# Attention score maxima of the last four heads, taken one pipeline step later, with all working banks in one ring

## The reference

```
x = x + layernorm(attention(layernorm(x)))
x = x + layernorm(ffn(layernorm(x)))

attention, for each batch and head (64-row blocks; d = 16):
  q, k, v = heads(x @ Wq.T + bq), heads(x @ Wk.T + bk), heads(x @ Wv.T + bv)
  first and last block of q: softmax over all of k
  the other blocks: softmax over the first, the last and the neighbouring blocks
  ctx = softmax(q k^T / sqrt(d)) v
ffn: abel = gelu(x @ abel_w + b); logits = x @ gate_w + b; the top two experts per token,
  each gelu(x @ w1 + b1) @ w2 + b2, weighed, rotated by three matrix exponentials and mixed with abel
```

## Time and profile before

| | |
|---|---|
| Median of 3 runs | 1895.45 us (1894.34 to 1897.08) |
| Span of the profiled execution | 1898.1 us |
| PE busy | 1572.6 us (83%) |
| DVE busy | 1247.2 us (66%) |
| ACT busy | 902.9 us (48%) |
| POOL busy | 706.7 us (37%) |
| Mean granted TensorE clock | 0.948 of full speed |

### The profile page before, as it was taken

One profiled execution on the slowest core, in us unless ns is written; L12 is line 12 of the kernel. 1 busy time (PEld: TensorE's weight loads), 2 busy tenths in 40 slices (PEclk: granted clock), 3 DMA queues, 4 the chain that ended last, 5 costly groups with the idle time before them and its releaser, 6 DMA issues. The chain is left out here.

```text
span 1898.1 us, 33342 instructions
## 1 busy us (share of the span) xinstructions
PE 1572.6 (83%) x10429; PEld 1070.8 (56%) x10430; DVE 1247.2 (66%) x3665; ACT 902.9 (48%) x1769; POOL 706.7 (37%) x716
## 2 busy tenths in 40 slices
PE   3988898888888888889888888749999999999700
PEld 1534455454455455545445545548888888888600
DVE  5656767877777787777778673426565555655377
ACT  1145656755756656666666656213333332323234
POOL 0011224324423423432433333414444444445458
PEclk9899999999999999999999999869999999999955
DMA  3331343353244245325424422755655656656387
GB/s 95 111 112 43 93 134 103 102 161 124 96 147 155 88 126 159 111 93 162 131 70 157 143 69 90 245 157 99 145 125 116 142 105 141 134 104 123 45 287 245
DMA packets 184011, 241.46 MB, mean 127 GB/s; under 512 B 23048, under 2 KB 154512, under 8 KB 183760
## 3 DMA queue, kind: packets, MB, share of 16 engines
q1 hardware_dynamic: 157008, 203.57, 33.6%
q0 software_dynamic: 26880, 36.33, 11.5%
HBM read 133.40 MB, written 105.91 MB: 126 GB/s over the span
## 5 line engine op out<-in xcount | busy, mean ns | idle before, releaser
L949 ACT ACTIVATE pexp<-scT 128x512 f32<-128x512 f32 x768 | 439.8, 600 | 322.2 <-PE scT L736 313.3
L1109 DVE TENSOR_REDUCE mx<-work 128x1 f32<-128x320 f32 (+2 forms) x1024 | 492.1, 549 | 48.5 <-PE work L716 46.1
L1599 POOL DMA_INDIRECT y_rows<-rows_add,row_of x144 | 226.8, 1575 | 296.1 <-DMA y_rows<-rows_add,row_of 211.3
L716 PE MATMUL work<-w 126*128 126x320 bf16 (+4 forms) x1280 | 265.1, 299 | 42.9 <-DVE mx L1109 33.6
L736 PE MATMUL scT<-w 128*128 128x192 bf16 (+3 forms) x1536 | 271.7, 275 | 28.2 <-ACT pexp L949 27.3
L1631 PE MATMUL h_ps<-inT,w1c 128*128 128x256 f32 x1152 | 263.6, 382 | 2.4 <-DVE inT L1683 2.4
L1644 PE MATMUL o_ps<-w,hT 128*128 x1152 | 260.4, 379 | 0.0
L1631 PEld LDWEIGHTS h_ps<-inT,w1c 128*128 128x128 f32 x1152 | 220.6, 192 | 33.8 <-issue 3.3
L1574 ACT ACTIVATE rows_add<-rows_out,row_share 128x257 f32<-128x257 f32 x144 | 65.6, 503 | 355.4 <-DVE rows_out L1699 281.7
L1644 PEld LDWEIGHTS o_ps<-w,hT 128*128 128x128 f32 x1152 | 213.4, 190 | 26.1
L736 PEld LDWEIGHTS scT<-w 128*128 128x128 bf16 x1536 | 122.8, 97 | 169.9 <-ACT pexp L949 111.2
(11 more groups left out here) (174 smaller groups left out, 2115.3 us busy)
## 6 DMA issues: line engine op xcount, KB each, us to landing
w<-split_spill SPq DMA_DIRECT2D x384, 128.0 KB, 2.9
split_spill<-split SPq DMA_DIRECT2D x64, 384.0 KB, 3.0
rows_in<-z_rows SPq DMA_DIRECT2D x72, 265.0 KB, 5.7
y_rows<-pre SPq DMA_DIRECT2D x16, 514.0 KB
y<-y_rows SPq DMA_DIRECT2D x16, 514.0 KB, 7.0
x_rows<-x SPq DMA_DIRECT2D x16, 512.0 KB, 2.6
abel_rows<-pre SPq DMA_DIRECT2D x16, 512.0 KB
abel_in<-abel_rows SPq DMA_DIRECT2D x16, 512.0 KB
```

What stands on the lines that cost most here:

```text
L716: ins = nc.tensor.matmul(work[t][:, at:at + hi - lo], tile(qst[par][0:K_SCORE, h, :], t), kst[par][0:K_SCORE, h, lo:hi], start=True, stop= ...
L949: nc.scalar.activation(pexp[:, (q * GROUP + n) % NPB, :], scT[n % 2][:, :], ACT.Exp, scale=DH ** -0.5).then_inc(s_exp, 1)
L1109: nc.vector.reduce_max(mx[:, c:c + 1], work[t][:, 0:n], AX_X).then_inc(w_free[t], 1)
L1599: pool.indirect_dma_start(kept.y_rows, bass.IndirectOffsetOnAxis(ap=row_of[n][:, r:r + 1], axis=0), rows_add[n % 2][:, r, :], None, comput ...
```

## The change

The maxima of heads 0 to 11 (`EARLY`, 48 units) are spread over quads 3 to 10, six in each. Of the last four heads' 16 units four stand in quad 11, and the other twelve are done in the next step: one behind each projection, two in quad 0, three in quad 1 and three in quad 2 (`LATE_AT`). `mx` is turned in two pieces, both into the bank `turn`: that of the 12 early heads in quad 11, and that of the four late heads in quad 3 of the next step, each with its own copy on ACT, its own subtraction on DVE and its own two DMAs of SP. The first score of a step waits for the early rows, the first score of head 12 (quad 9) for the late rows. On ACT the copy of the early piece stands ahead of the gelu.

The four working banks become one ring: `order_of` lists all uses of a step in PE's order, and use number i goes to bank i % 4 and waits for use number i - 4.

```diff
+EARLY = 12
+LATE_TURN_AT = 3
+LATE_AT = [("end", 1), ("end", 2), ("end", 3), ("end", 3),
+           ("proj", 0), ("proj", 1), ("proj", 2), ("proj", 3),
+           ("quad", 0, 3), ("quad", 0, 3), ("quad", 1, 3), ("quad", 1, 3), ("quad", 1, 3),
+           ("quad", 2, 1), ("quad", 2, 2), ("quad", 2, 3)]
...
-            units = [(h, t) for h in range(HEADS) for t in range(NT)]
-            some = units[max(q - B_FROM, 0) * len(units) // (QUADS - B_FROM):
-                         max(q - B_FROM + 1, 0) * len(units) // (QUADS - B_FROM)]
+            units = [(h, t) for h in range(EARLY) for t in range(NT)]
+            span = QUADS - 1 - B_FROM
+            if not B_FROM <= q < QUADS - 1:
+                return []
+            some = units[(q - B_FROM) * len(units) // span:(q - B_FROM + 1) * len(units) // span]
             third = -(-len(some) // 3)
...
+        def late(*where):
+            units = [(h, t) for h in range(EARLY, HEADS) for t in range(NT)]
+            return [unit for unit, at in zip(units, LATE_AT) if at == where]
...
+            seq = []
...
+            for m in range(4):
+                if here(s, 0):
+                    seq.append(("project", m))
+                if here(s, 1):
+                    maxima(s - 1, late("proj", m))
             if here(s, 3):
-                for k in range(KC):
-                    banks[Z_BANK[k]].append("z")
+                seq.extend(("z", k) for k in range(KC))
             for q in range(QUADS):
-                if here(s, 0):
-                    if q < V_QUADS:
-                        banks[2 + q].append("value")
-                    for n in range(1, GROUP):
-                        for h, t in fill(q, n):
-                            banks[t].append(("max", h))
+                for n in range(GROUP):
+                    if here(s, 0) and q < V_QUADS and n == 1:
+                        seq.append(("value", q))
+                    if here(s, 0):
+                        maxima(s, fill(q, n))
+                        if q == QUADS - 1:
+                            maxima(s, late("end", n))
+                    if here(s, 1):
+                        maxima(s - 1, late("quad", q, n))
                 if s == 0 and q == V_QUADS - 1:
-                    for n in range(SERIES_FIRST, len(SERIES) + 1):
-                        for i in range(NROT):
-                            banks[i].append(("series", n))
+                    seq.extend(("series", n, i) for n in range(SERIES_FIRST, len(SERIES) + 1) for i in range(NROT))
...
+        AT = {}
+        for s_, what_ in [(s_, what_) for s_ in range(-1, B + 3) for what_ in order_of(s_)]:
+            AT[s_, what_] = len(AT) % 4, len(AT) // 4
+        def bank(s, *what):
+            return work[AT[s, what][0]]
+        def full(eng, s, *what):
+            w, turns = AT[s, what]
+            eng.wait_ge(w_full[w], turns + 1)
+        def freed(eng, s, *what):
...
+        def reduced(eng, b, part):
+            units = [(h, t) for h in ((11,), (15,))[part] for t in range(NT)]
+            for h, t in units:
+                freed(eng, b + part, "max", b, h, t)
...
+            def put_maxima(par, b, part):
+                sp.wait_ge(s_m2[part], b + 1)
+                heads = slice(EARLY, HEADS) if part else slice(0, EARLY)
+                for n in range(N_MAX):
+                    r = MAX_ROW + n
+                    sp.dma_start(qst[par][r:r + 1, heads, :].rearrange("o h (t c) -> o (h t) c", c=P),
+                                 mrow[part][:, n, :]).then_inc(s_mrow[part], 16)
...
+                if here(s, 1):
+                    put_maxima(1 - par, s - 1, 1)
...
-                    freed(sp, s, 0, "turn")
-                    for part in range(N_MAX):
-                        r = MAX_ROW + part
-                        sp.dma_start(qst[par][r:r + 1, :, :].rearrange("o h (t c) -> o (h t) c", c=P),
-                                     mrow[:, part, :]).then_inc(s_mrow, 16)
+                    put_maxima(par, s, 0)
...
-            def turn_max(b):
-                for t in range(NT):
-                    freed(pe, b, t, ("max", HEADS - 1))
-                use(b, 0, "turn")
+                filled(ins, s, "max", b, h, t)
+            def turn_max(b, part):
+                reduced(pe, b, part)
+                if part:
+                    pe.wait_ge(s_m2[0], b + 1)
+                    wait(pe, s_ctxn, b * NTOK)
+                else:
+                    wait(pe, s_ctxn, (b - 1) * NTOK)
+                    pe.wait_ge(s_xnT, min(b + 2, B) * KC)
                 plain(pe)
-                nc.tensor.transpose(work[0][0:NT * HEADS, 0:P], mx[:, :], ident_sb[:, :]).then_inc(w_full[0], 1)
...
+                    if attend:
+                        for h, t in late("proj", m):
+                            max_unit(s, s - 1, 1 - par, h, t)
...
+                        if attend and q == LATE_TURN_AT and n == 2:
+                            turn_max(s - 1, 1)
                         if n > 0 and proj:
                             for h, t in fill(q, n):
-                                max_unit(s, par, h, t)
+                                max_unit(s, s, par, h, t)
+                        if proj and q == QUADS - 1:
+                            if n == 3:
+                                turn_max(s, 0)
+                            for h, t in late("end", n):
+                                max_unit(s, s, par, h, t)
+                        if attend:
+                            for h, t in late("quad", q, n):
+                                max_unit(s, s - 1, 1 - par, h, t)
                         if attend and q > 0 and n == 1:
                             pv_quad(s - 1, 1 - par, q - 1)
...
-                if proj:
-                    turn_max(s)
...
-            def first_max(b):
-                full(act, b, 0, "turn")
-                wait(act, s_mrow, b * N_MAX * 16)
-                nc.scalar.copy(mrow[:, 0, :], work[0][0:NT * HEADS, 0:P]).then_inc(s_m1, 1)
+            def first_max(b, part):
+                act.wait_ge(s_mt[part], b + 1)
+                wait(act, s_mrow[part], b * N_MAX * 16)
+                nc.scalar.copy(mrow[part][:, 0, :], turn[0:mrow[part].shape[0], 0:P]).then_inc(s_m1[part], 1)
...
+                    if attend and q == LATE_TURN_AT:
+                        first_max(s - 1, 1)
...
+                if proj:
+                    first_max(s, 0)
                 if routes:
                     abel(s - 3, 1 - par)
                     if attend and s < B:
                         nc.scalar.activation(warm[:, :], kept.neg_half[:, 0:1], ACT.Exp)
-                if proj:
-                    first_max(s)
...
+                def behind(*where):
+                    if attend:
+                        for h, t in late(*where):
+                            maximum(s, s - 1, h, t)
...
+                    behind("proj", m)
...
+                behind("quad", 0, 3)
...
+                behind("quad", 1, 3)
...
-                                maximum(s, h, t)
+                                maximum(s, s, h, t)
+                    if q == 2:
+                        for n in range(1, GROUP):
+                            behind("quad", 2, n)
+                    if attend and q == LATE_TURN_AT:
+                        second_max(s - 1, 1)
+                    if proj and q == QUADS - 1:
+                        for n in range(1, GROUP):
+                            for h, t in late("end", n):
...
```

308 lines of the change are left out of this document (150 added, 158 removed).

## The result

After the change the kernel takes 1811.72 us (median of 4 runs, 1810.62 to 1814.69); in the same job the kernel before took 1894.89 us (1893.08 to 1897.08). The ratio is 0.9558, with a 95% interval of 0.9536 to 0.9580: 83 us less, where 60 were forecast. The profiled execution has a span of 1808.8 us.

What follows compares the result with a forecast made beforehand. PE's order with its holes bounds the step, 6.2 of 8.2 us of waits being DVE behind in the maxima. 6 even steps x 3.2 + 7 odd x 5.1 + 5.6 + 6 + 4 - 1.5 = 69.0, less 9: 60 us, 1835; range 1788 to 1868.

Steps and rivals of the forecast that it cites:

- The sum for quads 4 to 11: Quads 4 to 11 of a middle step: 29.9 us in an even step (4.6 gained), 32.4 in an odd (6.7 gained).
- its start of quad 4: Quad 4 starts 32.1 us after the last exponential instead of 30.7: 1.4 us lost, 1.6 in an odd step.
- a worse clock: Rival: new closely spaced PE holes cost one more clock fall in each of 15 steps, 25 us: 1860; chance 0.10.
- All holes close: Rival: DVE's waits and the clock's falls vanish, 6.6 us a step, 99 in 15 steps: 1790; chance 0.11.
- The sign that the projections start within 0.3 us of the last exponential: Step's start: projections within 0.3 us of the last exponential would show the forecast right.
- third projection: Projection phase: PE waits 0.85 us for the first projection's bank, a new wait.
- first dense tile: Dense part: new 1.1 us wait for the second value projection's bank, which DVE evacuates 0.9 later.
- second: Dense part: the second dense tile waits 1.0 us for the first reduction of quad 1, a new wait.
- quad 3's fifth and sixth unit: Quad 3: the fifth unit waits 0.9 us for the first, behind the routing, where it waits 1.2 now.
- behind the statistics: Quads 4 to 11: 0.8 us of DVE's waits kept behind the statistics of quad 8.
- The late rows: Quad 9, head 12's score: rows land in 2.2 us with 13 us of room, so costed at nothing.
- The ring that binds PE to the slowest reader: Rival, third projection to second dense tile: nine uses each wait 1.0 us, a step loses 2 us: 1925; chance 0.09.

Runs made afterwards that it cites:

- the kernel with the transposes alone: Changed kernel with all 64 units in their own step and banks by kind; only the two-piece transpose ahead of the values stays: 1866.13 us, ratio 0.9846.
- the ring alone: Changed kernel with all 64 units back in their own step, ring and two-piece transpose kept: 1827.29 us, ratio 0.9642.
- Behind 1.20 us: Changed kernel with PE also waiting for DVE's subtraction of the early rows before the last quad's values: 1818.40 us, ratio 0.9608.
- behind 1.46 us: Changed kernel with units in their own step, ring kept, PE waiting for the last head's reductions before the last values: 1846.52 us, ratio 0.9725.
- Behind 3.13 us: Changed kernel with PE waiting for DVE's early-row subtraction and ACT's gelu before the last quad's values: 1866.81 us, ratio 0.9835.

## Why the prediction was right and wrong

The time was right: 1811.7 lies in the range 1788 to 1868, and faster had 0.88. It lies below the 1815 to 1855 that the forecast had for its own errors, 23 us under the middle. The mechanism was only half right. The parts as they measured:

| | units in their own step | units moved |
|---|---|---|
| banks by kind | 0.9846 | 1.0101 |
| ring | 0.9642 | 0.9558 |

From 1 to 0.9846 is the order at the step's end, some 28 us, 10.75 of them the clock's falls; from there to 0.9642 the ring, 39 us; and the moved units, after which the change is named, give 16 us, or cost 49 where the ring is absent. The two don't add up, one is the condition of the other: with the units moved the ring is worth 103 us (1.0101 to 0.9558).

**The part of the mechanism that was wrong** is the cause given for DVE's waits: "DVE is behind there because from quad 3 on it has some seven units in a quad". With the same seven and the ring DVE holds PE up for 2.3 us, not 7.0 (2.4, 1.85, 1.6, 0.8 and 0.3). The waits were those of a bank whose last use was a unit just issued, while other banks stood free: three of the rotation and one of z, 2.8 us in an even step of the kernel with the transposes alone, which the ring makes 0.2. What is left with the ring stands behind blocks of other work on DVE (0.93 us behind the routing, 1.14 in quad 9). I took a queue for a rate. The numbers to compare were there: 0.49 us for a unit and seven in a quad make 3.4 us, and a quad took 34.5 / 8 = 4.3 us before. With all its other work DVE was busy for 31.2 of 34.5 us in quads 4 to 11 of step 8 before, 91%, and with the ring and the same units for 31.05 of 33.05, 94%: near its limit, but most of PE's waits went without any of its work being taken away.

**The middle steps.** The sum for quads 4 to 11 had 4.6 and 6.7 us of gain from the moved units. In step 8 they take 30.6 us (61.7 - 31.1), 3.9 less than the 34.5 before. But the sum has to hold for the whole step, and there moving gives nothing: steps 3 to 14 take 759.2 us with the ring and the units in their own step, and 758.6 us with them moved. Quad 4 of step 8 shows why; with the units in their own step it begins here, 28.35 us after the last exponential (544.65):

```profile
573.00 0.38 PE L784 MATMUL scT<-w 128*128 128x320 bf16 x2
```

So the step is 28.35 + 33.05 us with the units in their own step, and 31.1 + 30.6 with them moved. Moving gives 2.45 us from quad 4 on and costs 2.75 ahead of it, in twelve units and new waits (0.37, 0.24 and 0.58 us). The prediction compared its start of quad 4, 32.1, with the 30.7 of the kernel before and counted 1.4 as lost; it did not see that the order at the step's end and the ring by themselves bring it to 28.35.

**Where moving pays** is in steps 0 to 2: 186.8 us with the units in their own step, 171.5 moved. Step 0 gives 5.3 of it (forecast 5.6: twelve reductions fewer, on DVE, which bounds this step), step 1 5.7 and step 2 4.4. Part of the last two is the clock: with the units in their own step it is at 0.95 and 0.97 in them, with them moved at 1.00 in both. The 16 projection matmuls of step 1 took 8.72 us there, and four times 1.9 moved, and the values behind PE's wait for a DMA took 1.94 us in each of the two steps where 1.08 is full speed. PE is busy 3.5 and 1.9 us less in the two steps with as many units, so the clock is up to about 5 of the 15.3 us. Of the waits, PE's for ACT's exponentials go from 4.5 to 2.5 us and from 4.6 to 3.1, and a wait of 1.4 us for a DMA in step 2 goes; why these shrink was not tested. In these steps DVE has no routing yet, and after the change it is busy for only 38 to 44 of 56 to 58 us, where in a middle step it is for 50 of 62. The run with only batches 0 to 2 moved shows it from the other side.

**The terms one by one** (us less than before; the second column is the profiled steps with the lower clock taken out):

| | forecast | measured |
|---|---|---|
| step 0 | 5.0 | 7.3 |
| step 1 | 5.4 | 5.9 |
| step 2 | 3.4 | 8.0 |
| steps 3 to 14 | 42.6 | 49.5 |
| step 15 to `experts` | 3.0 | 2.3 |
| clock | 0 | 12.2 |
| ahead of step 0 and in `experts` | 0 | 4.1 |
| sum | 59.4 | 89.3 |

The sum of the right column is that of the two profiled spans; by the medians it is 83, since the one profiled execution lay 3.2 us above its median and the other 2.9 below. The clock is the largest miss: in the kernel before the first projections of seven of the steps from 2 on took 4.82 to 5.40 us where others took 3.70 (the earlier trace rows have one of each), 10.75 us in all, and in step 1 it was 1.5 more; after the change none does. The prediction took 1.7 off for it in one odd step as a disturbance and priced a worse clock as a rival; a better one is named in "All holes close", but has no term in any sum. In step 2 I had 4 by analogy and no view: its waits before (1.9 for the transpose, 1.6 for the rotation, 1.3 for a DMA) add up to more, and its 8.0 holds a second fall of the clock, outside the projections, which the table leaves in. The values behind the wait for the DMA show it, 1.93 us and not 1.08:

```profile
196.48 1.93 PE L753 MATMUL pv<-pexp,vaug 128*32 128x192 f32 x24
```

**The signs.** No wait stands ahead of the transpose of the early maxima, the steps are near the 62.5 and 65 us named, even steps gain less than odd ones, and ACT has no hole from 561.94 to 573.98, through quads 5 and 6. The sign that the projections start within 0.3 us of the last exponential did not come (1.06 us), and it did not fit the prediction's own walk, in which the values start at 0.1 and come first; they start at 0.05.

**The new waits** came in their places and smaller than expected: third projection 0.37 (0.85), first dense tile 0.24 (1.1), second 0.58 (1.0), quad 3's fifth and sixth unit 0.41 + 0.29 (0.9), behind the statistics 0.89 + 0.29 (0.8). ACT's first evacuation came at 4.40 and not at 5.0, which is most of the first difference. Quad 4 starts at 31.1 (558.11 - 526.99), forecast 32.1, before 30.7. The steps took 61.7 and 64.8 where 62.6 and 65.0 were forecast. The late rows cost nothing, as said, though they land in 4.4 us and not in 2.2.

**The rivals.** The clock did not get worse: 1.00 in the middle steps of after and of the ring alone. The Trainium skill, "TensorE: Matmul & The Clock Gate", section on cycling through PSUM banks, tells of a kernel that cycles through its banks, leaves PE small idle times, and has its clock go back and forth. The middle steps of after do not agree with it: they have a four-bank ring, holes of 0.24 to 0.89 us, and a clock of 1.00. The ring that binds PE to the slowest reader was priced at 3 us of waits a step and is the other way round: it is the largest part of the gain. The price in that rival, "each of nine uses waits 1.0 us", has its like in the kernel with banks by kind and moved units, where the first dense tile waits 2.25: the danger was in the moving, and the ring takes it away. That all holes close did not come: 5.2 us of waits are left in step 8; the version with ten units moved and the statistics later goes on to 2.8 (1.8 for DVE, 0.7 and 0.3 for ACT).

**What the moved units are good for otherwise.** With the statistics in quad 10 the moved version gains 0.9% (0.9558 to 0.9471) and the other loses 0.3% (0.9642 to 0.9676), if anything. With six units in a quad and four in the last the end of a step has room for DVE's other work; with seven there is none, and the wait moves into quad 11. That this is the reason is read from the rows at 607.90 to 611.51, and not tested by itself.

**What stays open.** Why the clock falls where it does: see below. And why six late units in quad 11 are better than four: the dense tiles' waits (0.82 us in a step) go, and some of those for ACT's exponentials (1.8 to 1.1), which is more than the 1.35 gained, and which unit of the sixteen makes it was not tried alone.

## What to carry to other kernels

A list of waits of one engine on another says that a reader is late, not that it is overloaded: compare the reader's time for a stretch, all its work counted, with the issuer's before moving work off it, and look whether the waiting instruction's buffer was the only one that was taken. Where several kinds of work share a few buffers, number the uses in the order of issue and take the buffers in turn; here that alone was worth 39 us of 1894 with every unit in its own step, and moving work without it made the kernel slower. Take a change with several parts apart before naming its cause: the part that gave it its name was the smallest, 16 us on top of the other two.

## What the runs showed of the hardware

TensorE's clock fell behind holes of PE, but the length of a hole alone did not tell whether it would. Behind 1.20 us and behind 1.46 us, in every step from 2 on, the projections ran at full speed (four matmuls in 1.99 us, eight in 3.70); in step 1 of the same two runs, behind 1.17 and 1.47 us, eight took 5.26 and 6.17. Behind 1.85 us, the same in the kernel before at the end of every step from 1 on, they took 4.82 to 5.40 us in seven steps and 3.70 in the others. In the kernel with banks by kind and moved units 2.25 us stand ahead of the first dense tile in even and odd steps alike; eight of its matmuls took 2.03 us in step 8 and in five others of the 13 from 3 to 15, and 2.64 to 3.71 in the other seven, 3.13 in step 9. Behind 3.13 us the projections were slow in every step from 4 on. But with 0.95 and 0.29 us, two and a half us ahead of the projections, they were slow in three steps too (4.63 to 4.72), and at 3.70 in the other steps with the same holes; in the version with ten units moved and the statistics in quad 10, which has 0.76 to 1.06 and 0.29 us there, they were slow in none. I had expected falls behind holes of the size that the kernel before has, and none behind smaller ones. What else decides is not shown by any of these runs.
